# Correlation layers on one core: the convolution moved half a slot back, the correlation cut into quarters on VectorE

## What is computed

```
fn = feature / max(norm, EPS); fp = pad(fn, 2 on each side)
vol[cc*5 + r] = sum over channels of fp[:, :, r:h+r, cc:w+cc] * fn
out = relu(einsum('bihw,oi->bohw', concat([feature, vol]), conv_w) + conv_b)
```

## Time and profile before

| | us |
|---|---|
| median of 3 executions (570.29 to 570.53) | 570.47 |
| profiled execution, its own time | 571.38 |
| its span, first to last instruction | 569.5 |
| PE (TensorE matmul) busy | 502.5 |
| DVE (VectorE) busy | 408.0 |
| ACT (ScalarE) busy | 258.7 |
| POOL (GpSimd) busy | 165.4 |
| mean granted TensorE clock | 0.974 of full speed |

### The profile page before, as it was taken

How to read it: one execution, slowest core, us unless ns; L and a number is a source line. 1 busy time by engine, 2 the same in 40 slices (tenths; PEclk the granted TensorE clock), 3 DMA queues, 4 the chain that set the end, 5 groups by cost and what they waited for, 6 DMA issues and landing times.

```text
span 569.5 us, 7778 instructions
## 1 busy us (share of the span) xinstructions
PE 502.5 (88%) x2888; PEld 284.8 (50%) x2888; DVE 408.0 (72%) x828; ACT 258.7 (45%) x350; POOL 165.4 (29%) x135
## 2 busy tenths in 40 slices
PE   0357779999999989998999989998999989998996
PEld 0246337454564646454464636455464646454442
DVE  4879696786869588785969588785958778572442
ACT  1343454644546363643545364543646263543332
POOL 3354625023140504114140503214040503214240
PEclk9976989999999989999999989999999999999999
DMA  8764202223133812455043712356041512334403
GB/s 332 265 208 129 70 1 75 73 54 95 30 117 138 262 43 73 132 199 186 14 133 122 268 54 72 114 199 206 9 137 75 181 39 71 114 121 136 145 37 148
DMA packets 49885, 69.43 MB, mean 122 GB/s; under 512 B 6248, under 2 KB 39016, under 8 KB 49848
## 3 DMA queue, kind: packets, MB, share of 16 engines
q1 hardware_dynamic: 46008, 63.42, 33.1%
q0 software_dynamic: 3840, 5.52, 4.1%
HBM read 33.21 MB, written 35.71 MB: 121 GB/s over the span
## 4 chain that ended last, share of the span: by engine, by line
PE 34%; DVE 23%; issue 14%; POOL 14%; DMA 9%; ACT 5%; DVEq 0%; POOLq 0%
PE conv_ps L442 24%; DVE xs L792 5%; PE gram_ps L467 5%; DMA xs<-in_x_dram 4%; POOL corr L383 3%; POOL mirror L378 3%; DVE v L678 3%; POOL corr L381 3%; PE conv_ps L449 3%; DMA rows_dram<-rows 3%; DVE vol L689 2%; ACT act_out L594 2%; DMA out_dram<-xs 2%; DVE opnd L683 2%; DVE stats L625 2%
## 5 line engine op out<-in xcount | busy, mean ns | idle before, releaser
L442 PE MATMUL conv_ps<-opnd,wh 128*128 128x512 f16 x512 | 195.9, 383 | 0.2 <-ACT act_out L594 0.2
L442 PE MATMUL conv_ps<-opnd,whh 128*128 128x512 f16 x512 | 196.0, 383 | 0.0
L442 PE MATMUL conv_ps<-opnd,wl 128*128 128x512 f16 x512 | 195.9, 383 | 0.0
L594 ACT ACTIVATE act_out<-conv_ps,bias,wdown 128x512 f32<-128x512 f32 x128 | 97.4, 773 | 118.9 <-PE conv_ps L449 117.5
L792 DVE TENSOR_TENSOR xs<-xs,act_out 128x512 f32<-128x512 f32 x128 | 92.2, 736 | 44.8 <-ACT act_out L594 44.5
L467 PE MATMUL gram_ps<-opnd 128*128 128x256 f16 (+1 forms) x1024 | 111.1, 271 | 13.7 <-DVE opnd L683 11.7
L467 PEld LDWEIGHTS gram_ps<-opnd 128*128 128x128 f16 x1024 | 98.8, 100 | 27.6 <-issue 14.2
L625 DVE BATCH_NORM_STATS2 stats<-xs 128x6 f32<-128x512 f32 x128 | 78.3, 679 | 25.1 <-DMA xs<-in_x_dram 19.1
L359 POOL DMA_DIRECT2D mirror<-rows_dram x16 | 10.5, 659 | 273.3 <-DMA rows_dram<-rows 273.3
L683 DVE SCALAR_TENSOR_TENSOR opnd<-opnd,v 128x1024 f16<-128x1024 f16 x64 | 80.8, 1266 | 10.3 <-POOL v L390 4.1
L442 PEld LDWEIGHTS conv_ps<-opnd,whh 128*128 128x128 f16 x512 | 50.3, 98 | 61.8 <-issue 2.1
(11 more groups left out here) (67 smaller groups left out, 245.9 us busy)
## 6 DMA issues: line engine op xcount, KB each, us to landing
xs<-in_x_dram SPq DMA_DIRECT2D x32, 512.0 KB, 4.7
band_dram<-band SPq DMA_DIRECT2D x64, 256.0 KB, 2.3
out_dram<-xs SPq DMA_DIRECT2D x32, 512.0 KB, 2.9
skew<-band_dram SPq DMA_DIRECT2D x16, 532.0 KB, 4.0
opnd<-in_L_conv_conv_w_dram SPq DMA_DIRECT2D x2, 1074.0 KB, 12.5
rows_dram<-rows SPq DMA_DIRECT2D x16, 131.6 KB
mirror<-rows_dram POOLq DMA_DIRECT2D x16, 112.1 KB, 2.3
rn_far<-rows_dram POOLq DMA_DIRECT2D x16, 112.1 KB, 3.8
```

Source lines behind the costliest of these rows:

```text
L442: pe.matmul(conv_ps[:, g % 4, :], w[:, l, t, m * P:(m + 1) * P], opnd[:, slot, part, t, n * HALF:(n + 1) * HALF], start=(t == 0 and w is w ...
L594: act.activation(act_out[:, g % 2, :], conv_ps[:, g % 4, :], ACT.Relu, bias=bias[:, l, m:m + 1], scale=wdown[:, l, m:m + 1]).then_inc(relu, 1)
```

## The change

What it does, in the order of the code:

- **Order of units.** Four images of layer 0, the same four of layer 1, then the other four. The ring of x has 5 places; layer 1's raw weights lie in the fifth until image 4 is loaded (slot 4).
- **Slots.** From slot 3 on, slot k has products of unit k, then groups 4 to 7 of unit k-2 (j = 0 to 3), then groups 0 to 3 of unit k-1 (j = 4 to 7). There are 18 slots instead of 17. Slots before 3 are written out one by one on each engine. Average after the second pair of products; neighbours at j = 2; turn at j = 6.
- **First products** (unit 0) are taken tile by tile, into conv_ps, as the tiles come.
- **Correlation** on VectorE, on 100 partitions x 256 elements (each displacement in four quarters), in five operations, at the start of the next slot behind `unit_affine`. The rows themselves are now read back as a view too (`own`). Views are 7 transfers (rn_far in four), rows to DRAM are 2. High and low part of the volume are made in quarters (`corr_h`) and put in place by three transfers; `vol` is double.
- **GpSimd** has the head's work (constants, weights, doubled tiles of units 0 to 2) and otherwise issues views and volume transfers. For units 0 and 1 SyncE issues the views.
- **ScalarE** makes the doubled tiles from unit 3 on (VectorE did), both halves of the rows' copy (VectorE had one), no more volume copies. On it, the square root for the next unit stands between band copies 0 and 1, its first tile between 1 and 2.
- **VectorE** takes statistics of unit k+2 at j = 4 to 6; it no longer waits for GpSimd's constants at its start.
- **SyncE** sends the first two output tiles before the bands, and the other tiles, the loads and (in slot 4) image 4 between bands and rows.
- Layer 1's weights: scale at the end of slot 3, turned in slot 4 at j = 3 to 7. GpSimd's reserve for descriptors is 4096 instead of the default.

The core of the diff:

```diff
 def unit_layer(u):
-    if u <= LEAD:
-        return 0
-    return 1 if u % 2 or u > UNITS - LEAD - 2 else 0
+    return u // TEAM % LAYERS
...
+        STEADY = 3
+        SLOTS = UNITS + 2
+        TURN_AT = 6
+        NORM_AT = 2
+        W1_MAX_SLOT, W1_SLOT, W1_AT = 3, 4, 3
+        V2_ON_POOL = (0, 1, 2)
         HOLD = 1
+        EARLY = 2
+        def group_of(k, j):
+            u = k - 2 if j < 4 else k - 1
+            return (u, (j + 4) % GROUPS) if valid(u) and u > 0 else None
+
+        def views_from_dram(eng, k):
+            eng.wait_ge(rows_out, 32 * (k + 1))
+            wait(eng, corr_step, CORR_STEPS * k)
...
+            eng.dma_start(mirror[:, 0:run],
+                           bass.AP(rows_dram, base + (NS + 1) * PSZ, [[B_PITCH + PW, NS], quarters, [1, run]])
+                           ).then_inc(arrived, 16)
+            eng.dma_start(rn_own[:, 0:run],
+                           bass.AP(rows_dram, rn_row + R * PW + R, [[0, NS], quarters, [1, run]])
+                           ).then_inc(arrived, 16)
+            eng.dma_start(own[:, 0:run],
+                           bass.AP(rows_dram, base + R * PW + R, [[PSZ, NS], quarters, [1, run]])
+                           ).then_inc(arrived, 16)
+            for c in range(QUARTERS):
+                eng.dma_start(rn_far[c:QPARTS:QUARTERS, 0:run],
+                               bass.AP(rows_dram, rn_row + c * QRUN, [[1, S], [PW, S], [1, run]])
+                               ).then_inc(arrived, 16)
+
+        def volume_in(eng, k):
+            eng.wait_ge(corr_step, CORR_STEPS * (k + 1))
+            wait(eng, conv, GROUPS * (k - 1))
+            for at, part in ((0, 0), (32, 1), (64, 0)):
+                eng.dma_start(vol[at:at + NS, k % 2, :].rearrange("s (q n) -> s q n", q=QUARTERS),
+                               corr_h[:, part, :]).then_inc(vol_in, 16)
...
 SyncE
+            for k in range(STEADY, SLOTS):
+                tiles_out(k - 2, (0, 1))
+                if valid(k):
+                    band_through_dram(k)
+                tiles_out(k - 2, (2, 3))
+                tiles_in(k - 2)
+                if k == W1_SLOT:
+                    sp.wait_ge(w_turned, LAYERS * (KT + 1))
+                    load(TEAM)
+                if valid(k):
+                    rows_to_dram(k)
 GpSimd
+            double_tiles(0, range(KT))
+            scaled_weights(0)
+            half_weights(0)
+            double_tiles(1, range(KT))
+            volume_in(pool, 0)
+            double_tiles(2, range(KT))
+            volume_in(pool, 1)
+            for k in range(EARLY, UNITS):
+                if k == W1_SLOT:
+                    half_weights(1)
+                views_from_dram(pool, k)
+                if k == W1_MAX_SLOT:
+                    scaled_weights(1)
+                volume_in(pool, k)
 TensorE, from slot 3
+                    for p in range(PAIRS):
+                        products(k, p)
+                        if p == 1 and valid(k + 1):
+                            average(k + 1)
+                for j in range(GROUPS):
+                    if k == W1_SLOT and j >= W1_AT:
+                        turn_weights(1, j - W1_AT)
+                    if j == TURN_AT and valid(k):
+                        turn(k)
...
+                    channels(u, g)
+                    if g == HOLD:
+                        for h in range(HOLD):
+                            volume(u, h)
+                    if g >= HOLD:
+                        volume(u, g)
 ScalarE, from slot 3
+                    band_out_of_psum(k, 0)
+                    if valid(k + 1):
+                        deviations(k + 1)
+                    band_out_of_psum(k, 1)
+                    if valid(k + 1):
+                        norm_tile(k + 1, 0)
+                    band_out_of_psum(k, 2)
+                    band_out_of_psum(k, 3)
+                    if valid(k + 1):
+                        double_tile(k + 1, 0)
+                        norm_tile(k + 1, 1)
+                        double_tile(k + 1, 1)
...
 VectorE, before slot 3 and from it
+            for t in range(KT):
+                stats_tile(4, t)
+            stats_done(4)
+            for g in range(4):
+                added(1, g)
+            for k in range(STEADY, SLOTS):
+                if valid(k + 1):
+                    unit_affine(k + 1)
+                if valid(k - 1):
+                    correlation(k - 1)
+                if valid(k + 1):
+                    low_tile(k + 1, 0)
+                    low_tile(k + 1, 1)
+                for j in range(GROUPS):
...
+                    if j == NORM_AT and valid(k):
                         neighbours(k)
+                    if j in (1, 2) and valid(k + 1):
+                        low_tile(k + 1, j + 1)
+                    if valid(k + 2):
+                        for t in {4: (0, 1), 5: (2,), 6: (3,)}.get(j, ()):
+                            stats_tile(k + 2, t)
+                        if j == 7:
+                            stats_done(k + 2)
+                    job = group_of(k, j)
+                    if job is not None:
+                        added(*job)
+                if k == W1_MAX_SLOT:
+                    scale_weights(1)
```

More of the change, by code:

```diff
@@ new lines, in first_products, with products @@
+            def first_products():
+                for t in range(KT):
+                    pe.wait_ge(high, t + 1)
+                    pe.wait_ge(low, t + 1)
+                    for p in range(PAIRS):
+                        for j in (2 * p, 2 * p + 1):
+                            for part in range(2):
+                                last = product(0, j, t, part)
+                        if t == KT - 1:
+                            last.then_inc(gram, 1)
+            def products(u, p):
+                if p == 0:
+                    pe.wait_ge(high, KT * (u + 1))
+                    pe.wait_ge(low, KT * (u + 1))
+                pe.wait_ge(band_sb, PAIRS * u + p - 1)
+                for j in (2 * p, 2 * p + 1):
+                    for t in range(KT):
+                        for part in range(2):
+                            last = product(u, j, t, part)
+                last.then_inc(gram, 1)
@@ new lines, in _ @@
+            average(0)
+            first_products()
+            for n in range(KT + 1):
+                turn_weights(0, n)
+            average(1)
+            pe.wait_ge(w_half, KT)
+            pe.wait_ge(w_low, KT)
+            channels(0, 0)
+            turn(0)
+            channels(0, 1)
+            pe.wait_ge(w_low, W_LOWS)
+            for g in range(2, 4):
+                channels(0, g)
+            for p in range(PAIRS):
+                products(1, p)
+            average(2)
+            for g in range(4):
+                volume(0, g)
@@ new lines, in _ @@
+            for g in range(4, GROUPS):
+                channels(0, g)
+                volume(0, g)
+            turn(1)
+            for p in range(PAIRS):
+                products(2, p)
+                if p == 1:
+                    average(3)
+            for g in range(4):
+                channels(1, g)
+            for g in range(4):
+                volume(1, g)
+            turn(2)
+            for k in range(STEADY, SLOTS):
+                if valid(k):
+                    if k == W1_SLOT + 1:
@@ new lines, in rectified @@
+            def rectified(u, g):
+                l, m = unit_layer(u), g // 2
+                act.wait_ge(conv, GROUPS * u + g + 1)
+                wait(act, x_sum, GROUPS * u + g - 1)
+                act.activation(act_out[:, g % 2, :], conv_ps[:, g % 4, :], ACT.Relu,
+                               bias=bias[:, l, m:m + 1], scale=wdown[:, l, m:m + 1]).then_inc(relu, 1)
+            deviations(0)
+            for t in range(KT):
+                norm_tile(0, t)
+            for p in range(PAIRS):
+                band_out_of_psum(0, p)
@@ L670, in unit_affine, with low_tile @@
                 dve.tensor_scalar(affine[:, 1, :, :], affine[:, 0, :, :], 2.0, None, ALU.mult).then_inc(gn_step, 1)
[L672 to L680 removed]
+            def low_tile(u, t):
@@ L794, in _, with added @@
-            slots(dve, step)
+            def added(u, g):
+                m, n = g // 2, g % 2
+                xt = xs[:, ring_slot(unit_batch(u)), m, n * HALF:(n + 1) * HALF]
+                dve.wait_ge(relu, GROUPS * u + g + 1)
+                dve.tensor_tensor(xt, xt, act_out[:, g % 2, :], ALU.add).then_inc(x_sum, 1)
+            for t in range(KT):
+                stats_tile(0, t)
+            stats_done(0)
+            unit_affine(0)
+            for t in range(KT):
+                low_tile(0, t)
@@ new lines, in _ @@
+            scale_weights(0)
+            for t in range(KT):
+                stats_tile(1, t)
+            stats_done(1)
+            for n in range(KT):
+                low_weights(0, n)
+            unit_affine(1)
+            neighbours(0)
+            low_weights(0, KT)
+            for t in range(KT):
```

(24 more changed lines are left out.)

630 lines of the change are left out of this document (279 added, 351 removed).

## The result

| | before | after |
|---|---|---|
| median, measured together, us | 570.5 (570.29 to 572.42, 4 runs) | 546.48 (545.27 to 546.97, 4 runs) |
| span of the profiled execution, us | 569.5 | 544.9 |
| mean granted TensorE clock | 0.974 | 0.980 |

The ratio is 0.9569, with a 95% interval of 0.9543 to 0.9595. The forecast was 545.5 us, and 544.7 for the span. The total is right; several terms of its sum are not, and they cancel.

What follows compares the result with a forecast made beforehand. TensorE bounds the kernel, losing time to volume and neighbour waits. Head 95.5, slots 3 to 5 36, 35 and 34.5, ten slots 305, last groups 33.8, tail 4.9: 544.7, plus 1.0 for measurement: 545.5 us, range 536 to 554.

Steps and rivals of the forecast that it cites:

- What bounds it, and the floor: Steady slots: PE bounds, losing time to volume and neighbour waits and clock; floor 30.24 busy us per slot, unchanged.
- Part 1, the volume: Steady slots: volume lands 13.5 into the slot, asked for at 23.8; slack 10 us, removing 14.4 us of waits.
- The prediction's own sign of being wrong: Steady slots: DVE's first correlation multiply starting later than 9 into its slot behind a view.
- part 3: Steady slots: ACT carries 19.0 and DVE 22.6 us, both fit; thin cover costs nothing; a slot takes 30.5.
- Part 2, the neighbours: Steady slots: neighbours done by +21, turn at +23.8, so the 12.4 us of waits go.
- the cover is thin: Steady slots: DVE ends about 2 us after PE; views may land 3.3 us later than computed before PE feels it.
- Part 4, the head: Before slot 3: first products end at 25.0 instead of 32.5; a walk with neighbour and volume stops reaches turn 2's end at 95.5.
- Part 5, the stalls after it: Slots 3 to 5: late DVE work, second weights and late views make them 36, 35 and 34.5 us.
- Sum: Whole kernel: head, slots 3 to 5, ten steady slots, last groups and tail give a 544.7 us span, 545.5 us measured.
- Thin cover: Rival, steady slots: view issues at 1.2 instead of 0.6 make PE stop; eleven slots at 31.7 to 32.2, 560 us; chance 0.17.
- No stalls in the head: Rival, head and switch of weights: DVE and ACT quicker than drawn, about 12 us of stalls fall, 533 us; chance 0.11.
- POOL held up by DVE: Rival, 11 slots: DVE operations block POOL's issues, views land 8.9 later, 5.6 past the cover; 607 us; chance 0.06.

Runs made afterwards that it cites:

- turn4: The changed kernel with the turn before group j=4 instead of j=6, all else the same: 569.55 us, ratio 0.998.
- whole6: The changed kernel without the half-slot shift from slot 3 on (whole convolution of unit k-1 in slot k), turn kept at j=6: 592.77 us, ratio 1.0395.
- whole4: As whole6, but with the turn at j=4: 602.92 us, ratio 1.0574.
- late8: The changed kernel with eight GpSimd fills of a spare tile ahead of each unit's views: 569.83 us, ratio 0.9969.
- dbldve: The changed kernel with the doubled tiles of units 3 to 15 back on VectorE instead of ScalarE: 558.9 us, ratio 0.978.
- corrpool: The changed kernel with the correlation of units 2 to 15 on GpSimd, still in quarters on 100 partitions: 547.77 us, ratio 0.9592.
- head123: As head1, with unit 1's correlation earlier, unit 2's neighbours and root later, and layer 1's weight scale behind slot 3's correlation: 540.19 us, ratio 0.9454.
- head1: The changed kernel with the statistics of unit 4 moved into VectorE's idle time ahead of slot 3: 546.14 us, ratio 0.9563.
- whole4pool: As whole4, with the correlation of units 2 to 15 on GpSimd in the same quarters: 609.62 us, ratio 1.0664.
- dblrows: As dbldve, with SyncE issuing the rows to DRAM ahead of the loads of x: 549.13 us, ratio 0.9608.

## Why the prediction was right, and where it was not

**What bounds it, and the floor.** Right: PE, and a slot is its busy time once the waits are gone.

**Part 1, the volume.** Right in quiet slots. POOL's first view in the slot from 296.10 was forecast at 29.3 and is issued 29.6 in; the seven took 4.3 (said 4.2), and DVE's five operations 2.0 (said 2.0):

```profile
325.71 0.67 POOL L262 DMA_DIRECT2D mirror<-rows_dram  x1 [14.68 <-DMA rows_dram<-rows]
...
327.55 2.44 POOL L272 DMA_DIRECT2D rn_far<-rows_dram  x4
...
334.71 0.71 POOL L281 DMA_DIRECT2D vol<-corr_h  x1 [4.72 <-DVE corr_h L815]
```

The slack is 10 us there, and smaller in the slots with loads, where the views come at 10.5: the rows leave SyncE in time but take 7.9 to POOL's next issue; in quiet slots it is 3.6 to 3.8, and the forecast had 3.1 for two transfers, from the 2.3 of one in the earlier trace rows:

```profile
261.81 0.46 SPq L346 DMA_DIRECT2D rows_dram<-rows  x1
...
269.76 0.67 POOL L262 DMA_DIRECT2D mirror<-rows_dram  x1 [19.45 <-DMA rows_dram<-rows]
```

I had priced that transfer from one moment without a load in front of it and used it for all slots. The prediction's own sign of being wrong, a correlation that starts later than 9 behind a view, did come, in slots 5 to 9 (9.5 to 14.0); it had no cost, for the reason under part 3.

**Part 2, the neighbours.** Right: said 21, measured 19.5 to 20.3 in slots 6 to 14, 23.4 in slot 5, turn at 23.6 (said 23.8). That the turn's place alone carries 23 us with the shift, and only 10 without, was not in the prediction; turn4, whole6 and whole4 show it.

**Part 3, who carries the rest.** Two sizes off, and one step wrong. A steady slot is 30.08, not 30.5: the average's 0.3 does not appear, and the floor is 30.05, not 30.24. The work is the same; turn4, with one stop per slot, shows 30.23 busy again. A matmul counts 0.38 busy at a pitch of 0.22, so each stop adds some 0.16 of tail to the busy time, and I read the floor from a slot with a stop. ACT's 18.1 and DVE's 20.8 per slot were said as 19.0 and 22.6; I used busy means, where back-to-back operations start about 0.1 us closer together than they last (two sums have 1.29 busy, start to start 0.6). The wrong step is "the cover is thin: views may land 3.3 us later": the edge lies near 14.2, not 9.7. DVE does end its last sum 1.7 behind PE (357.90, slot end 356.20; said 2), but the statistics that PE asks for are done before that sum, at 355.82, and DVE is busy 20.8 of 30.05, so its idle time takes up most of a lateness. What runs out first is the turn. late8 shows 12.4 free, slot 5 shows 14.0 free, and dbldve's 13.95 costs only because DVE then needs 11.7 behind it.

**Part 4, the head.** Here the first step failed. PE reached the points of the walk at 51.9 (said 51), 61.8 (61) and 76.6 (75), so the head up to slot 2 stands. The step "half of unit 1 with a second, shorter wait and turn 2 to 95.5" gave slot 2 20.5 us; it took 25.3, with the waits of 2.14 and 2.20 above and a clock of 0.93. The average of unit 3 and its wait I had not drawn at all. Slot 3 started 6.3 late. How the loss is shared out is one profile's (turn4 and corrpool, with the same head, start slot 3 at 104.66 and 105.66 and need 34.6 and 33.1 for it); that slot 5 starts 9 late is not, it is 175.2 to 176.3 in all three.

**Part 5, the stalls after it.** Slot 3 took 36.3 (said 36), slot 4 37.4 (35). The second step that failed is slot 5, 30.05 instead of 34.5: the views did come late there, at 14.0, even later than the 12.6 said, but the edge of 9.7 that should have made them cost 4 us does not exist.

**Sum.** +6.3 at slot 3, +0.3 in it, +2.4 in slot 4, -4.5 in slot 5, -4.1 in ten slots (175.56 + 30.05 to the end of unit 15's slot at 506.50), -0.3 from there to the end: 0.2 in all, which is 544.9 - 544.7. The total is right partly by luck: terms that came 9.0 longer and terms that came 8.9 shorter cancel. That the waits go and the steady slots fall to PE's busy time is not luck.

**Rivals.** *Thin cover*: the premise, issues of 1.2, did not come. Views made 4.9 later by other means (late8) give 570, but by load slots alone and not by each slot, as the rival had it. *No stalls in the head*: head123, with part of them gone, is at 540. *POOL held up by DVE*: the 140 issues of the kernel after from slot 3 on took 0.61 to 0.79, and the 23 of them that began while DVE ran a low tile 0.68 to 0.70. The Trainium skill's rule ("SBUF — State Buffer", section "A bandwidth-pool intuition that's wrong (but worth ruling out)"), about 3.1 us beside a DVE copy, was not met here: no issue of the kernel after began beside a long copy, and most issues took a little over the 0.62 that it gives for one alone. The kernel after has no doubling on DVE, a scale of 1024 elements with one input; dbldve has. There the three issues of a volume, the last of them beside such an operation, take 2.35 together, and without one 2.05 (kernel after, from 279.07):

```profile
255.63 2.35 POOL L281 DMA_DIRECT2D vol<-corr_h  x3 [6.28 <-DVE corr_h L819]
...
256.96 0.81 DVE L797 TENSOR_SCALAR v<-xs,affine 128x1024 f32<-128x1024 f32 x1
```

That is 0.3 us for the one issue, where the rival needed 0.5 on each before it would decide.

## To carry to other kernels

When a chain through several engines is too long for its place, two moves can be worth more together than their sum: here the later turn gives 10 us alone and 23 beside the shifted convolution, and both are needed to beat the kernel before. Price each queue's order, not only its load: the correlation stood behind the scale and shift on DVE, the rows behind the loads on SyncE, the lengths behind a ReLU on ACT. The first two decided a run; the third is read from a trace alone. A filled wait pays only as far as the next chain moves with it: what head1 won in the head was lost in slot 5, whose views came no earlier. And a wait in one profile is compared with the same stretch in other kernels that share its code, before a cause is put to its length.

## What the runs showed of the hardware that was not expected

- The clock does not answer to every stop, and the length of a stop alone does not tell. Slots of turn4 with one PE wait of 1.48 keep 1.00 and 30.23 us busy. In whole4pool each of nine slots has one wait, of 2.29 to 2.31, at the same place: seven show 0.95 and 31.8 to 32.1 busy, two show 1.00, this one and the slot from 482.93:

```profile
244.32:276.91 32.59, 30.30 (x179) 17.01 (x178) 19.35 (x45) 18.36 (x24) 10.27 (x17) 1.00 0.60 205
```

So against 30.05 a wait of 2.3 cost 4.1 to 4.4 us or 2.5 to 2.7, and one of 1.5 cost 1.7. In dbldve the slot from 271.22, with waits of 0.57 and 2.27, stayed at 1.00, and the one from 304.58, with 0.57 and 1.94, fell to 0.95. What decides between them is open.
- From the issue of `rows` to POOL's next issue it took 7.3 to 8.5 us in slots where SyncE had just issued loads of x, 3.5 to 3.8 in the others, and 4.3 to 4.4 in dblrows, where the loads stand behind the rows.
- In corrpool a two-input operation of the correlation (100 x 256) on POOL takes 0.72 alone, and 1.31 to 1.71 where it began while DVE ran a low tile, also of two inputs. A low tile that began during such an operation took 1.25 to 1.78 instead of 1.22. POOL's issues of transfers began beside low tiles too and were not longer for it. In the schedule with slack this made no measurable difference.
